# A two-layer conditioned attention kernel: an opening of its own for item 0, and the bias network spread over items 0 to 2

## What is computed

```python
# layer 0, x: (32, 128, 512); null_kv: (2, 64); attn_bias: (16, 128, 128)
xn = layernorm(x, g_in)
q = (xn @ Wq).reshape(b, n, H, DH).transpose(0, 2, 1, 3) * scale
k, v = split(xn @ Wkv)                  # one k and one v for all heads
k, v = concat([nk, k]), concat([nv, v]) # a null key and value in front
sim = einsum('bhid,bjd->bhij', q, k) + concat([null_col, attn_bias])
attn = softmax(where(causal_or_masked, neg, sim))
out = layernorm(attn_out @ Wo, g_out)
# layer 1
q = l2norm(q) * q_scale ; k = l2norm(k) * k_scale ; sim = ... * 8
def rel_pos_bias(n, w0, b0, g0, w1, b1, g1, w2, b2, dtype):
    pos = jnp.arange(-n + 1, n, dtype=dtype)[:, None]
    h = jax.nn.silu(ln(pos @ w0 + b0, g0))
    h = jax.nn.silu(ln(h @ w1 + b1, g1))
    h = h @ w2 + b2
x = x + layer0(x)
x = x + layer1(x)
```

## Time and profile before

| | us |
|---|---|
| median of 3 runs | 1352.89 (1351.42 to 1353.7) |
| the profiled execution | 1354.02 |
| its span in the trace | 1352.2 |
| PE busy | 1285.5 |
| DVE / ACT / POOL busy | 1103.6 / 860.5 / 753.8 |
| mean granted PE clock | 0.99 |

### The profile page before, as it was taken

The page is one execution under the profiler, slowest core; times in us unless marked ns, Lnnn a source line. Parts: engine busy times, 40 slices in busy tenths (PEclk is TensorE's granted clock), DMA queues, the critical chain, the costliest instruction groups (busy, mean ns, idle before and its releaser), DMA issues.

```text
span 1352.2 us, 28917 instructions
## 1 busy us (share of the span) xinstructions
PE 1285.5 (95%) x8152; PEld 1185.0 (88%) x8152; DVE 1103.6 (82%) x2964; ACT 860.5 (64%) x3245; POOL 753.8 (56%) x1332
## 2 busy tenths in 40 slices
PE   0689999999999999999999999999999999999997
PEld 0488999999999999999888999999999999999996
DVE  3657778777777877777799998999999999899985
ACT  1366666666666666666757667666666666666663
POOL 1734444444444444444466677767766776776673
PEclk9799999999999999999999999999999999999999
DMA  5761111111011111101101011011101101110101
GB/s 153 218 147 49 47 47 36 34 47 47 23 47 47 38 32 47 47 23 47 48 24 48 25 47 47 31 39 47 47 23 47 47 27 43 47 45 24 47 32 40
DMA packets 45347, 67.46 MB, mean 50 GB/s; under 512 B 8832, under 2 KB 17024, under 8 KB 45312
## 3 DMA queue, kind: packets, MB, share of 16 engines
q1 hardware_dynamic: 43504, 64.66, 15.8%
q10 hardware_dynamic: 1808, 2.39, 0.5%
HBM read 48.16 MB, written 18.87 MB: 50 GB/s over the span
## 4 chain that ended last, share of the span: by engine, by line
PE 88%; DVE 4%; DMA 2%; POOL 2%; issue 1%; SPq 1%; ACT 1%; POOLq 0%; DVEq 0%; ACTq 0%
PE bank_q L1093 29%; PE bank_y L1218 24%; PE bank_s L1093 12%; PE bank_o L1093 10%; PE bank_p L1185 6%; PE bank_t L1158 4%; PE bank_t L1126 3%; SPq L323 1%; DMA x_in<-in_x 1%; DMA wo_raw<-in_L_cond_Wo 1%; POOL wo_l L485 1%; PE bank_t L1163 1%; DVE wq_l L766 0%; DVE qt_l L901 0%; SPq L364 0%
## 5 line engine op out<-in xcount | busy, mean ns | idle before, releaser
L655 ACT ACTIVATE p_raw<-s_sb,neg_m 128x130 f32<-128x130 f32 (+1 forms) x1024 | 371.9, 366 | 141.9 <-DVE neg_m L959 139.8
L511 POOL TENSOR_TENSOR p_sb<-p_raw,rden 128x256 f32<-128x256 f32 x256 | 158.0, 617 | 358.5 <-DVE rden L965 358.4
L1093 PE MATMUL bank_q<-wq_h,xt_h 128*128 128x384 f32 x768 | 268.6, 350 | 5.2 <-ACT q_nat L616 3.3
L1093 PE MATMUL bank_q<-wq_h,xt_l 128*128 128x384 f32 x768 | 260.5, 339 | 0.0
L1093 PE MATMUL bank_q<-wq_l,xt_h 128*128 128x384 f32 x768 | 260.4, 339 | 0.0
L501 POOL TENSOR_TENSOR bias_g<-bias,mask_row 128x260 f32<-128x260 f32 x256 | 178.5, 697 | 111.0 <-DVE s_sb L952 109.3
L1218 PE MATMUL bank_y<-wo_h,ot_h 128*128 128x512 f32 x512 | 219.0, 428 | 0.0
L1218 PE MATMUL bank_y<-wo_h,ot_l 128*128 128x512 f32 x512 | 202.2, 395 | 0.0
L1218 PE MATMUL bank_y<-wo_l,ot_h 128*128 128x512 f32 x512 | 202.0, 394 | 0.0
L655 ACT ACTIVATION_READ_ACCUMULATOR p_raw<-s_sb,neg_m 128x1 f32 x1024 | 192.3, 188 | 0.0
L952 DVE TENSOR_TENSOR s_sb<-bank_s,bias_g 128x392 f32<-128x392 f32 x256 | 143.1, 559 | 38.9 <-PE bank_s L1093 38.9
(11 more groups left out here) (118 smaller groups left out, 3137.1 us busy)
## 6 DMA issues: line engine op xcount, KB each, us to landing
x_in<-in_x SPq DMA_DIRECT2D x32, 256.0 KB, 2.7
x_res<-in_x SPq DMA_DIRECT2D x32, 256.0 KB, 2.6
x_mid<-y_out SPq DMA_DIRECT2D x32, 256.0 KB, 2.0
x_in<-x_mid SPq DMA_DIRECT2D x32, 256.0 KB, 2.8
x_res<-x_mid SPq DMA_DIRECT2D x32, 256.0 KB, 2.7
out_x<-y_out SPq DMA_DIRECT2D x32, 256.0 KB, 2.0
wq_raw<-in_L_cond_Wq SPq DMA_DIRECT2D x4, 768.0 KB, 9.0
wo_raw<-in_L_cond_Wo SPq DMA_DIRECT2D x1, 2048.0 KB, 9.1
```

Of the source, the lines that this page charges most:

```text
L511: e.tensor_tensor(to[:, 0:2 * P].rearrange("p (e j) -> p e j", e=2), low_blocks(of)[:, :, 2:LOW], r[:, 0:2, :].broadcast_to([P, 2, P]), AL ...
L655: last = e.activation(p_raw[:, g % 2, lo:hi], s_sb[:, g % 2, lo:hi], ACT.Exp, bias=neg_m[:, h:h + 1], accum_out=esum[:, h:h + 1])
L1093: last = e.matmul(out, a, b, start=(k == 0), stop=(k == len(passes) - 1))
```

## The change

`stream` starts at step 0. What steps -3 to -1 did is written out per engine.

- SP: x of item 0 first, then `load_wq(0)`, three nulls, `load_bias0`, the mask of layer 0, x of item 1, three rows of the network, `load_wo(0)`, the network's other five loads, x of item 2. The table store, `load_wq(1)`, `load_wo(1)` and `load_bias1` all stand in `between(2)`.
- ACT issues four small loads and begins with `project_weights(0, 0)`. The halves of `wo_h` move into step 0.
- DVE: item 0's statistics and the weight splits come first; the network's first layer is spread between the q, k stages of item 0. The first half of `wo_l` moves from POOL to DVE in step 0. The network's second layer is spread over steps 0 (`net_second_layer`) and 1, its table over the ends of steps 1 and 2.
- POOL issues the nine other small loads after `masked_bias((0, 0), 2)`. The second half of `wo_l`, the second inverse deviation, the null key's norm and the layer-1 nulls come in `between(1)`.
- PE begins with x of item 0; the network's first transposes and its 512 x 512 product move into step 0.

```diff
-    straight(-3, FIRST)
+    straight(0, FIRST)
@@ SP
             def between(n):
-                if n == -2:
-                    load_wq(0)
-                if n == -1:
-                    load_wo(0)
-                    load_bias0()
...
-                if n == 0:
-                    for p in range(3):
-                        e.wait_ge(wq_ready[p], 1)
-                    load_wq(1)
-                if n == 1:
-                    e.wait_ge(wo_ready, 2)
-                    load_wo(1)
+                if n == 2:
                     e.wait_ge(net_step, TABLE)
                     e.dma_start(table, table_sb.unsqueeze(1).broadcast_to([H, P, 2 * P])).then_inc(table_stored, 16)
-                if n == 2:
+                    load_wq(1)
+                    for half in range(2):
+                        e.wait_ge(wo_ready[half], 1)
+                    load_wo(1)
                     e.wait_ge(table_stored, 16)
                     load_bias1()
 
+            load_x((0, 0))
+            load_wq(0)
...
+            load_bias0()
+            load_mask(0)
+            wait(e, xn_ready, (0, 0))
+            load_x((0, 1))
+            for dst, src in ((w0_b, w0[0]), (b0_b, b0), (g_b[0], g0)):
+                net_row(dst, src)
+            load_wo(0)
+            for p in range(3):
+                e.wait_ge(wq_ready[p], 1)
+            net_load(w1_sb[:, :, :], w1.rearrange("(c p) n -> p c n", p=P))
...
+            wait(e, xn_ready, (0, 1))
+            load_x((0, 2))
@@ POOL
             def between(n):
-                if n == -2:
-                    causal_masks()
-                    place_nulls()
-                if n == -1:
-                    for c in range(OC):
...
-                    net_deviation(VE2)
-                    mask_bias0()
+                if n == 1:
+                    output_weights(0, 1)
+                    net_deviation(VE2)
+                    null_norm()
+                    place_nulls(1)
...
+            never_seen()
+            causal_masks()
+            inverse_deviations(item_of(-3))
+            mask_bias0()
+            inverse_deviations(item_of(-2))
+            net_deviation(VE1)
+            e.wait_ge(null_bias_loaded, 16 * LAYERS)
+            place_nulls(0)
+            for g in (1, 0, 2):
+                masked_bias((0, 0), g)
+            load_small()
+            inverse_deviations(item_of(-1))
             stream(e, step, between)
@@ ACT
+                on(0, start_output, 0)
                 on(1, q_out, 0)
...
+                on(1, start_copy, 1, TP1, TCOPY1)
...
                 on(0, exps, 3)
+                on(0, start_output, 1)
                 on(0, split_pt, 1)
...
                 on(0, split_pt, 3)
+                on(1, start_copy, 2, TP2, TCOPY2)
...
+            project_weights(0, 0)
+            split_xt(first)
+            project_weights(0, 1)
+            project_weights(0, 2)
+            q_out(first, 0)
+            q_out(first, 1)
+            q_out(first, 2)
             net_silu(GAIN1, EXP1)
-            project_weights(0, 0)
-            net_copy(TP1, TCOPY1)
-            project_weights(0, 1)
+            split_qt(first, 0)
+            split_qt(first, 1)
+            split_kt(first)
@@ DVE, step
+                on(0, net_table)
                 on(1, split_xt)
...
                 on(2, ln_apply)
+                on(0, net_second_norm)
...
+                on(0, net_second_silu, [0, 1])
                 on(0, split_pt, 1)
+                on(0, start_output)
...
+                on(0, net_second_silu, [3])
+                on(0, net_second_layer)
                 means_variances(at)
@@ DVE, ahead of stream
+            x_stats(first)
+            means_variances(item_of(-3))
+            ln_apply(first)
+            project_weights(0, 0)
+            split_xt(first)
+            project_weights(0, 1)
+            project_weights(0, 2)
+            x_stats(second)
+            means_variances(item_of(-2))
+            take_mask(first)
             net_first_layer()
+            first_null()
+            ln_apply(second)
+            q_scale_out(first, 2)
+            net_norm(RSTD1, CEN1, g_b[0])
+            split_qt(first, 0)
+            net_silu(EXP1, PLUS1, REC1, [0])
+            split_qt(first, 1)
+            net_silu(EXP1, PLUS1, REC1, [1])
+            split_kt(first)
+            x_stats(third)
+            means_variances(item_of(-1))
+            net_silu(EXP1, PLUS1, REC1, [2, 3])
@@ PE, step
+                on(0, net_table)
                 on(1, transpose_x)
-                on(1, start_product)
...
                 on(1, project, 1)
+                on(0, net_first_transposes)
                 on(0, transpose_p, 0)
                 on(0, scores, 3)
+                on(0, net_product)
                 on(1, project, 2)
-                on(0, start_table)
...
                 on(0, transpose_p, 3)
+                on(0, net_second_transposes)
+            transpose_x(first)
+            for p in range(3):
+                project(first, p)
+            transpose_q(first, 0)
+            transpose_q(first, 1)
+            transpose_k(first)
```

More of the change, by code:

```diff
@@ L107, in straight @@
                 between(n)
-            step(lambda d, n=n: ((n + d) // B, (n + d) % B) if 0 <= n + d < N else None)
-    straight(-3, FIRST)
+            step(item_of(n))
+    straight(0, FIRST)
     for layer in range(LAYERS):
@@ L401, in between @@
                     e.wait_ge(table_stored, 16)
                     load_bias1()
+            load_x((0, 0))
+            load_wq(0)
+            for half in range(2):
+                rows = slice(half * DH, (half + 1) * DH)
+                null(null_k_col[rows, :], cond[0:1, :].rearrange("a d -> d a"))
+            null(null_v[:, :], cond[1:2, :].broadcast_to([P, DH]))
+            load_bias0()
[4 more added lines that the diff above has]
+                net_row(dst, src)
@@ L404, in _ @@
+            for layer in range(LAYERS):
+                e.dma_start(g_out_sb[:, layer, :], row(g_out[layer]).broadcast_to([P, D])).then_inc(g_out_loaded, 16)
+            load_mask(1)
             stream(e, step, between)
@@ L665, in split_ot @@
                 wait(e, pv_psum[half], m)
+                if is_item(m, 0, 0) and half == 0:
+                    e.wait_ge(small_loaded, 16 * SMALL_LOADS)
                 wait(e, wo_half[half], m, -1)
```

309 lines of the change are left out of this document (163 added, 146 removed).

## The result

The changed kernel takes 1384.87 us (median of 4 runs, 1384.58 to 1386.78), the kernel before, on the same chip, 1352.62 (4 runs, 1351.42 to 1353.7). The ratio is 1.0243, 95% interval 1.0226 to 1.0259. It is slower by 32 us, and the time lies 2.4 us above the 1382.5 predicted.

What follows compares the result with a forecast made beforehand. PE is nearly always busy, so only the opening and steps 0 to 2 can move: -29.3 + 14.6 + 14.3 + 30 = +29.6 us, giving 1382.5 as the median, range 1360 to 1396.

Steps and rivals of the forecast that it cites:

- What bounds it: Whole kernel: PE is busy 1285.5 of 1352.2 us, so only the opening and first steps, up to step 3's start, can move.
- A: Opening: step 0 starts at 33 us in place of 62.3, a gain of 29.3.
- B: Step 0: lasts 37.5 us in place of 22.9, a loss of 14.6, bounds 5 and 18.
- the nine DMAs on POOL: Step 0, first term of B: POOL's small loads delay group-3 bias and first normalise, +7.4 us.
- the other two terms: Step 0, in B: the 512 x 512 product moved into the step, +3.8 us, and the second half's latency chain, +3.4.
- The third term: Step 0's second half, in B: a latency chain over ACT, DVE and PE with wo and network work ahead, +3.4 us.
- C: Step 1: lasts 35.1 us in place of 20.8, a loss of 14.3, bounds 6 and 18.
- D: Step 2: lasts 51.1 us in place of 21.1, a loss of 30, with DVE waiting 30.5 for x of item 5.
- R1: Step 2: table alone lands in 7.6 us, not 23; D falls by 15.4, time 1367; chance 0.08.
- R2: Steps 0 and 1: POOL's DMAs issue at once, added work finds cover; B 4, C 8, time 1366; chance 0.10.
- R3: Faster: R1 and R2 together, with weights passing beside the table; -9.8 us, time 1343; chance 0.07.
- R4: Opening held by DMA at 200 GB/s, POOL's DMAs dearer than SP's; A -21, B 18, time 1394; chance 0.07.

Runs made afterwards that it cites:

- second profile: The changed kernel as it is, run and profiled again on the chip of the follow-ups: 1385.58 us, ratio 1.0237.
- A1: Changed kernel with x of item 1 and the network's three rows loaded ahead of bias and mask: 1384.68 us, ratio 1.0226; same edit on B3: 1337.64.
- B1: Changed kernel with POOL's nine small loads issued in the opening, not between the bias of groups 2 and 3: 1382.82 us, ratio 1.0219.
- B3: B2 with wo_h half 1, wo_l half 0, the split 512 x 512 product and second-layer bias and statistics moved to idle places: 1338.58 us, ratio 0.9884.
- B2: D5 and B1 together, with POOL's wo_l of step 1 split into pairs and the null key's work later: 1344.47 us, ratio 0.9940.
- D1: Changed kernel with SP's wait on table_stored and the bias reads moved behind x of item 5: 1381.21 us, ratio 1.0188.
- D4: Kernel before, with only table store, layer-1 weights, wait and bias reads put into SP's between(2): 1387.14 us, ratio 1.0249.
- D5: Changed kernel with a halved table behind x of item 5 and the rest of the queue spread behind x of two later items: 1349.5 us, ratio 0.9961.

## Point by point: why the prediction was right, and where it was off

**What bounds it** held: PE's idle time at the start was the only thing that moved, and behind the start of step 3 only 0.1 us did.

**A, 29.3 predicted, 26.9 measured.** In the second profile it is 28.5. What was mis-sized is the transfers' time. DVE had x of item 1 at 20.3 and not 18, and the three rows at 24.1 and not 20.5, as these two rows of the first profile show:

```profile
20.28 0.69 DVE L912 BATCH_NORM_STATS2 moments<-x_in 128x6 f32<-128x512 f32 x1 [3.24 <-DMA x_in<-in_x]
...
24.11 0.15 DVE L878 CAST pos<-pos_i 128x1 f32<-128x1 int32 x1 [2.33 <-DMA p_sb<-in_L_cond_g]
```

The working had 377 GB/s for 4.2 MB, 3 to 5 us ahead of the first byte and a little for the slower bias rows. The first weights moved at 321 GB/s (5.2 to 8.5 us), but 170 moved from 11.7 to 15.6, when bias rows were under way, and 215 from 20.8 to 22.8, when the broadcast rows were; no run has either alone. That the rows end last was right, and step 0 starts 11.3 behind them, 12.5 in the working, which gave 1.2 of the 3.6 back. In the second profile the rows are there at 22.5, 1.6 earlier, and step 0 starts 11.3 behind them again; A1 shows the dependence too. The projections ended at 22.2 and not near 17, which cost nothing, as the rows came later still.

**B, 14.6 predicted, 11.2 measured.** In the second profile it is 9.6. The term mis-sized is the nine DMAs on POOL: +7.4 taken, and B1, which moves them out, shortens the step by 3.7 against the first profile and 2.0 against the second. One part of this is their length, 7.9 taken and 5.0 measured. The bounds were 3.5 and 7.9, and I took the upper end for a reason, the scattered columns, that the rows don't bear out: those of 64 x 1 elements took 0.52 to 0.54 behind the first, like the others. The other part is a slip: 7.9 and 0.7 with 2 of slack make 6.6 and not 7.4. What is left of the step's loss without this term is 7.5, where the other two terms had 7.2. The figure of about 1 us from the Trainium skill (DMA: Bandwidth & Descriptors, Latency and other measured facts) stands for the whole first byte; POOL was held for 0.52 to 0.78 for each, and the sum by the page, 9, would have been further off. The product, priced at 5.5, took 4.94 and, in the second profile, 3.65. The third term was right in kind, and B3 shows that by another placing of work nearly all of the step's loss can be had back.

**C, 14.3 predicted, 14.2 measured.** The total is right, its parts less so. POOL's block, 7.1 us long and 7.8 in the working, made PE stand 5.5, +6 predicted; when most of it left (B2), PE's idle time fell by 1.8 only, since other waits took its place. So that the sum of its six parts came out to 0.1 is in part luck. The table's chain at the turn of the steps was exact, 2.9 from the first transpose at 101.56 to 104.46:

```profile
101.56 0.63 PE L1193 MATMUL bank_t<-ident,y_out 128*128 128x128 f32 x4 [1.90 <-DVE y_out L873]
...
102.87 1.05 PE L1187 MATMUL bank_t<-y_out,w_sb 128*16 128x128 f32 x8 [0.69 <-ACT y_out L630]
...
104.46 0.66 PE L1227 MATMUL bank_t<-ident,xn 128*128 128x128 f32 x4 [0.54 <-DVE squares L907]
```

**D, 30 predicted, 32.4 measured, 35.1 in the second profile.** The step that decided the sign held by each of its parts: the table in 22.4 us (21 to 24 predicted), x behind weights and bias, and the one wait, 33.3 for 30.5. x was there 40.8 behind `y_finish`. Its terms were right: table 22.8 (23.4), weights 12.6 behind that (11.8), bias reads and x 5.4 (4.9), which makes 40.1 by the working's own numbers. The step that failed is that I took 38, the lower end of its "38 to 41". The order of the queue alone explains it (D1: 29 of 33; D4: the same wait without the rest of the change). On the Trainium skill's rule that descriptors are taken in ring order (DMA: Bandwidth & Descriptors, Queues, rings and completion order): the trace agrees, with 29.1 us for an x behind a table that it doesn't need. Here the issue itself was held as well, 16.7 us for three.

**The rivals.** R1 (a fast table) is out: alone on the engines it moves at 101 to 105 GB/s, and half of it takes half the time, 12.2. The 6.8 us that the prediction worked out from the Trainium skill (DMA: Bandwidth & Descriptors, Anatomy of one DMA) is an estimate by a fit for DMAs that POOL issues, and SP issues this store; the trace has 22.4. R2 was half right on POOL's DMAs and wrong on cover: it priced B and C at 12, they came to 25.4. R3 and R4 did not come about; that the changed opening can be made faster than the old needed other kernels, with half the table and its queue spread (D5, 0.996) and several moves of work besides (B3, 0.988).

**The sum** by the measured terms: -26.9 + 11.2 + 14.2 + 32.4 = 30.9, span 31.0. Errors of +2.4, -3.4, -0.1 and +2.4 (+0.8, -5.0, 0 and +5.1 in the second profile) largely cancel and leave 1.3 (0.8), so that the sum came this close is in part luck. The other 1.1 is 0.1 behind step 3, and that the medians are 32.2 apart and the spans 31.0, less the 0.3 by which the kernel before was quicker beside this one.

## What to carry to other kernels

Before an instruction is moved along a queue, list what stands behind it there and when that is wanted: a store that costs 1 us or so at one place (23.0 us in the shadow of two steps) costs 33 us two steps later, with the weights behind it and in front of one load of 256 KB. Price the rest of the queue until it is empty, too; to put the urgent load in front only moves the stall to the next one if the backlog is longer than a step. Work spread into a pipeline's first steps is free only in an engine's own gaps and not ahead of what the others wait for: between D5 and B3 only such places differ, and they are worth 10 to 11 us. And profile the same program twice before a difference of 2 us in one step is put down to an edit.

## What the runs showed of the hardware that I had not expected

- A store of 2 MB made from 16 partitions, each line written 128 times, ran at 101 to 105 GB/s alone on the 16 engines, and took 12.2 us for 1 MB and 22.4 for 2 MB. So it is slow by its shape, not by what runs beside it; which property of it does this (16 source partitions, lines of 1 KB) was not tried.
- With such a store queued ahead, the issue of the next loads on the same queue was held: 16.7 us for three (10.1 with half the table). With the store on ACT's queue SP's issues were held too, 4.92 and 4.44 us for ones that take 0.4 to 0.6.
- A small DMA issued by POOL held it for 0.52 to 0.57 us, the first for 0.78, with 64 x 1 and with 128 x 64 elements.
- In two executions of the changed kernel PE's instructions of step 2 took 21.1 us of busy time at a granted clock of 0.72 and 23.8 at 0.65, with the same idle time (32.4 us in both), and in step 0 its 512 x 512 product took 4.94 and 3.65 us. The clock of such a step differs from one execution of the same program to the next.
